# An adaLN block with a mixture of experts on one Trainium2 core: the hand-written orders around block 7's routing, and where the load of expert 1's weights stands

## The reference

```python
h = _layernorm(x, axis=-1) * (1 + cb) + sb
scores = jax.nn.softmax(xt @ router_w, axis=-1)              # 8 experts
expert_weights, expert_idx = jax.lax.top_k(scores, TOP_K)     # 2 of them
h = gelu(einsum('td,edf->tef', xt, w1)) * einsum('td,edf->tef', xt, v1)   # f = 704
y = einsum('tef,efd->ted', h, w2)
out = sum(expert_weights * y[chosen], axis=1) + bias
x = x + gb * out
```

## Time and profile before

| | us |
|---|---|
| median of 3 runs | 848.93 |
| lowest, highest | 848.23, 850.63 |
| profiled execution, its time | 848.34 |
| its span, first to last instruction | 846.2 |
| TensorE busy in the span | 818.6 (97%) |
| VectorE, GpSimd, ScalarE busy | 557.7, 485.8, 367.9 |
| mean granted TensorE clock | 0.996 of full |

### The profile page before, as it was taken

The page is one execution under the profiler, slowest core; times in us unless marked ns, Lnnn a source line. Parts: engine busy times, 40 slices in busy tenths (PEclk is TensorE's granted clock), DMA queues, the critical chain, the costliest instruction groups (busy, mean ns, idle before and its releaser), DMA issues.

```text
span 846.2 us, 18804 instructions
## 1 busy us (share of the span) xinstructions
PE 818.6 (97%) x5006; PEld 724.6 (86%) x5007; DVE 557.7 (66%) x1534; ACT 367.9 (43%) x681; POOL 485.8 (57%) x454
## 2 busy tenths in 40 slices
PE   8899999999999999978999999999999999999995
PEld 4679898988889879757999999999999999999994
DVE  6788777878876848775555655555655565565553
ACT  5884657565564525534224234224233242342221
POOL 2353645868685877569645646537537465383332
PEclk9999999999999999999999999999999999999998
DMA  8141050303021172327532432523324322222221
GB/s 281 34 113 50 2 181 9 119 26 102 14 90 45 58 233 62 142 78 199 153 47 40 137 45 37 150 44 113 68 38 137 51 37 44 38 38 38 38 45 25
DMA packets 49983, 67.64 MB, mean 80 GB/s; under 512 B 4944, under 2 KB 44240, under 8 KB 49936
## 3 DMA queue, kind: packets, MB, share of 16 engines
q1 hardware_dynamic: 36272, 47.71, 18.4%
q0 software_dynamic: 13664, 19.35, 12.2%
HBM read 43.51 MB, written 23.54 MB: 79 GB/s over the span
## 4 chain that ended last, share of the span: by engine, by line
PE 87%; POOL 3%; DVE 3%; issue 1%; ACT 1%; DMA 1%; another core or an unknown queue 0%; ACTq 0%; DVEq 0%; POOLq 0%
PE ps L614 24%; PE ps L616 24%; PE ps L615 24%; PE ps L776 5%; PE ps L742 2%; PE ps L715 1%; POOL routed L2009 1%; DMA out_rows<-y_moe,tok_moe 1%; PE ps L819 1%; PE ps L818 1%; PE ps L660 1%; PE ps L702 1%; PE ps L632 1%; PE ps L667 1%; POOL out_rows L2031 1%
## 5 line engine op out<-in xcount | busy, mean ns | idle before, releaser
L614 PE MATMUL ps<-split,xT_moe_hi 128*128 (+2 forms) x426 | 165.5, 388 | 0.1
L616 PE MATMUL ps<-split,xT_moe_hi 128*128 (+2 forms) x426 | 160.1, 376 | 0.0
L615 PE MATMUL ps<-split,xT_moe_lo 128*128 (+2 forms) x426 | 159.8, 375 | 0.0
L2021 POOL TENSOR_TENSOR y_moe<-y_moe 128x256 f32<-128x256 f32 x69 | 65.9, 956 | 122.8 <-DVE y_moe L1653 122.6
L1174 ACT ACTIVATE hidT_hi<-ps 128x768 fp32r<-128x768 f32 x70 | 56.9, 813 | 177.7 <-PE ps L776 168.6
L2031 POOL DMA_INDIRECT out_rows<-y_moe,tok_moe x71 | 111.1, 1564 | 28.9 <-issue 22.5
L1168 ACT ACTIVATE gelu_moe<-ps 128x704 f32<-128x704 f32 x71 | 53.8, 758 | 133.6 <-PE ps L616 126.9
L614 PE MATMUL ps<-split,hidT_hi 128*128 (+1 forms) x355 | 99.9, 281 | 1.3 <-DVE y_moe L1653 0.7
L615 PE MATMUL ps<-split,hidT_lo 128*128 (+1 forms) x355 | 100.1, 282 | 0.0
L616 PE MATMUL ps<-split,hidT_hi 128*128 (+1 forms) x355 | 99.9, 281 | 0.0
L1970 POOL TENSOR_TENSOR hid_lo<-hf_sb,hid_hi 128x512 fp32r<-128x512 f32 x48 | 67.1, 1399 | 50.8 <-ACT hid_hi L1146 50.7
(11 more groups left out here) (232 smaller groups left out, 1993.9 us busy)
## 6 DMA issues: line engine op xcount, KB each, us to landing
raw<-in_w SPq DMA_DIRECT2D x9, 1408.0 KB
x_moe<-routed SPq DMA_DIRECT2D x74, 132.5 KB
raw<-in_w SPq DMA_DIRECT2D x9, 640.0 KB
x_again<-in_x SPq DMA_DIRECT2D x8, 512.0 KB
out_rows<-x_again SPq DMA_DIRECT2D x8, 512.0 KB
x_sb<-in_x SPq DMA_DIRECT2D x7, 512.0 KB, 3.9
gu_raw<-in_gu_t SPq DMA_DIRECT2D x1, 1536.0 KB, 8.9
raw<-in_w SPq DMA_DIRECT2D x18, 64.0 KB
```

What stands on the lines that cost most here:

```text
L614: pe.matmul(dst, a_hi, b_hi, start=first, stop=False)
L615: pe.matmul(dst, a_lo, b_hi, start=False, stop=False)
L616: return pe.matmul(dst, a_hi, b_lo, start=False, stop=last)
L2021: g.tensor_tensor(y_moe[:, t.slot, 0, :], y_moe[:, t.slot, 0, :], y_moe[:, t.slot, 1, :], ALU.add)\
```

## The change

Six lists are edited; no computation is added or taken away but fills. SyncE: the load of expert 1 goes from ahead of the table's wait to behind the rows of tiles 5 to 8. TensorE: the fills in this part become fewer and stand elsewhere (27 before, 13 after); ranks 6 and 7 move ahead; hidden transposes and second product of tile 4 go ahead of tile 5's row transposes, out of `tile_step`. ScalarE: `router_exp(6)` goes ahead of gelu 1, the splits of expert 0 and the copies of block 7 change places with gelus. VectorE: `slots(6)` and `weigh(6)` follow block 7's statistics, `count(7)` moves behind `slots(7)` and `weigh(7)`, and the low splits of expert 0 move to the end.

```diff
@@ SyncE
             store_base(NBLK - 2)
-            load_weights(sp, 1, RAW_SLOT)
             sp.wait_ge(tab_ready, 1)
...
             for n in range(EARLY, EARLY + SLOTS):
                 load_by_table(Tile(n))
+            load_weights(sp, 1, RAW_SLOT)
             store_base(NBLK - 1)
             load_weights(sp, 2, 0)
@@ TensorE, tile_step
-                hid_transposes(t.near(-1))
-                if t.n > EARLY and not final(t):
-                    x_transposes(t.near(1))
+                if t.n > EARLY:
+                    hid_transposes(t.near(-1))
+                    if not final(t):
+                        x_transposes(t.near(1))
                 first_products(t, e)
                 if t.n == EARLY:
                     x_transposes(t.near(1))
-                second_product(t.near(-1), PICKED if t.n == EARLY else pe.snap(kept, min_val=0, max_val=E - 1))
+                else:
+                    second_product(t.near(-1), pe.snap(kept, min_val=0, max_val=E - 1))
@@ TensorE, list
             first_products(Tile(1), PICKED, AB[2:])
-            pe.wait_ge(gelu_r, 2)
-            fill(0, 3)
+            rank_tokens(6)
             x_transposes(Tile(2))
             second_product(Tile(0), PICKED)
-            rank_tokens(6)
+            pe.wait_ge(gelu_r, 2)
+            fill(0, 8)
             hid_transposes(Tile(1))
             first_products(Tile(2), PICKED, AB[:2])
-            pe.wait_ge(hid_r, 2)
-            fill(2, 4)
             h2_transposes(7, 0)
             first_products(Tile(2), PICKED, AB[2:])
             h2_transposes(7, 1)
+            x_transposes(Tile(3))
             router_logits(7)
-            x_transposes(Tile(3))
             second_product(Tile(1), PICKED)
-            fill(RING, 5)
+            rank_tokens(7)
             hid_transposes(Tile(2))
-            rank_tokens(7)
             first_products(Tile(3), PICKED, AB[:2])
+            first_products(Tile(3), PICKED, AB[2:])
             count_all()
-            first_products(Tile(3), PICKED, AB[2:])
-            fill(RING, 4)
+            x_transposes(Tile(4))
             second_product(Tile(2), PICKED)
-            x_transposes(Tile(4))
-            fill(RING, 4)
-            table_transposes()
-            pe.wait_ge(gelu_r, 4)
-            fill(0, 7)
             hid_transposes(Tile(3))
             first_products(Tile(4), PICKED, AB[:2])
+            table_transposes()
             first_products(Tile(4), PICKED, AB[2:])
             second_product(Tile(3), PICKED)
+            hid_transposes(Tile(4))
+            second_product(Tile(4), PICKED)
+            pe.wait_ge(gelu_r, 5)
+            fill(0, 5)
             x_transposes(Tile(5))
@@ ScalarE, list
             hidT_split(Tile(0))
+            router_exp(6)
             gelu(Tile(1))
             xT_split(Tile(2))
-            router_exp(6)
-            hidT_split(Tile(1))
             split_hi(act, 0, 0)
             split_hi(act, 0, 1)
+            hidT_split(Tile(1))
             h2_copy(7, 0)
+            gelu(Tile(2))
             h2_copy(7, 1)
-            gelu(Tile(2))
             xT_split(Tile(3))
+            split_hi(act, 0, 2)
             router_exp(7)
-            split_hi(act, 0, 2)
...
             gelu(Tile(4))
+            hidT_split(Tile(4))
             xT_split(Tile(5))
-            hidT_split(Tile(4))
@@ VectorE, list
             norm2_stats(7)
+            slots(6)
+            weigh(6)
             multiply(Tile(1))
             xT_rest(Tile(2))
             norm2_centre(7)
             norm2_scale(7)
-            slots(6)
-            weigh(6)
+            hidT_rest(Tile(1))
             gate_y(Tile(0))
             count(6)
-            hidT_rest(Tile(1))
             multiply(Tile(2))
             choose(7)
-            count(7)
             xT_rest(Tile(3))
-            take_gates(Tile(2), expert)
             slots(7)
             weigh(7)
             hidT_rest(Tile(2))
+            count(7)
             gate_y(Tile(1))
+            take_gates(Tile(2), expert)
+            multiply(Tile(3))
+            xT_rest(Tile(4))
             table()
-            split_lo(v, 0, 2)
-            xT_rest(Tile(4))
-            multiply(Tile(3))
-            split_lo(v, 0, 0)
-            table_out()
             hidT_rest(Tile(3))
             gate_y(Tile(2))
-            split_lo(v, 0, 1)
+            table_out()
             multiply(Tile(4))
-            xT_rest(Tile(5))
+            split_lo(v, 0, 0)
             take_gates(Tile(3), expert)
             gate_y(Tile(3))
+            hidT_rest(Tile(4))
+            split_lo(v, 0, 1)
+            xT_rest(Tile(5))
             take_gates(Tile(4), expert)
-            hidT_rest(Tile(4))
+            split_lo(v, 0, 2)
             take_gates(Tile(5))
```

## The result

The changed kernel takes 859.99 us (median of 4, 857.44 to 860.83) against 849.78 (848.23 to 850.8) of the kernel before on the same chip: ratio 1.0120, 95% interval 1.0094 to 1.0145, so 10 us slower, outside the forecast's range. The profiled execution took 860.83 us (span 858.7), the slowest of its four, and that of the kernel before 848.34, so the two traces lie 12.5 us apart and the medians 10.2.

The account below looks back on a forecast made before the run. Bound: the chain to tile 6's hidden transposes, then TensorE alone. Load issued 384.85 + 1.7 = 386.5, + 10.3 = 396.8, + 4.5 = 401.3 against 402.09, 0.8 us sooner: 848.1 against 848.93; 8-in-10 range 845.4 to 851.8.

Parts of the forecast that it names:

- late signals: TensorE's h2, logit and rank signals beside scatter 6: delay between 0 and 3.4 us, taken as 1.7.
- 0.3 planned: Second product 3 on TensorE was to wait 0.3 us for `gate_y(2)`.
- The load: Expert 1's load: issued at 386.5, landing 10.3 us later, then 4.5 us to tile 6's hidden transposes.
- Clock: Rival, chance 0.20: TensorE's clock falls in new gaps before second product 4 or hidden 6; total 850 to 852 us.
- mark of error: Sign of being wrong: a TensorE clock below 1.00 between 377 and 405 us.
- price of 2 to 4 us: Cost the clock rival, chance 0.20, put on top of the sum for half clock after a gap.
- the 5 or more: Sign of being right: ScalarE idle 5 us or more before L395, released by a DMA.
- The load is hidden: Rival, chance 0.10: load lands by 393, ScalarE doesn't wait, 4.3 to 6 us faster, 843 to 844.6.
- The gain of the order: Scatter 7 and tile 5's rows come sooner; some 3.5 us of the gain is lost waiting for the load.
- 396.1 without the load's wait: When TensorE would reach tile 6's hidden transposes if the load held nothing; 397.8 with late signals.
- planned 2.5: TensorE's wait ahead of second product 4, planned at 2.5 us.
- Choice 7: Block 7's choice on VectorE: takes 1.9 us, ends about 361.7 against 361.81; over 1 us off means wrong.

Follow-up runs that it names:

- e14: Changed kernel with at most two scatters in flight in blocks 6 and 7: 853.10 us, ratio 1.0036 to the kernel before.
- e3: Changed kernel with matmuls on ones added in TensorE's gaps: 855.53 us, ratio 1.0109 to the kernel before.
- e2: Kernel before with only the load of expert 1 moved behind the rows of tile 8: 852.26 us, ratio 1.0051.
- e12: Changed kernel with early load, early low split piece, two scatters in flight at most in blocks 6 and 7, no added matmuls: 848.77 us, ratio 0.9984.
- e8: Changed kernel with only one scatter of block 7 in flight at a time: 858.23 us, ratio 1.0111 to the kernel before.
- e11: Kernel before with only a limit of two scatters in flight in blocks 6 and 7: 852.29 us, ratio 1.0021.
- e1: Changed kernel with the load of expert 1 issued early again: 853.44 us, ratio 1.0079 to the kernel before.
- e13: Kernel before without its 27 fills between tiles 1 and 4: 848.98 us, ratio 1.0000.

## Why the prediction was wrong

- **The failed step: late signals, sized at 1.7 us.** The prediction took half of 3.4, between one row that showed 3.4 and the dense steps that showed 0.3. The changed kernel has 2.3 at the logits, 3.9 at second product 3 (6.2 in ScalarE's row), and 1.3 at the table, where VectorE waits 1.07 us on its own instruction before: 7.2 us on the path beyond the 0.3 planned, more than its upper bound of 3.4, since that was a bound for one signal, and the order has several behind each other. Limiting the scatters, and nothing else, gave back 7 of 10 us (e14). The load went out at 399.35 instead of 386.5, 12.8 us late, landed in 1.0 us less than forecast, and tile 6 came 11.8 us late.
- **The order was the multiplier.** The prediction saw scatter 6 come to lie over the logits. It did not ask the same of scatter 7, moved to 368 to 378, over tile 3's hidden transposes and the table. In the kernel before the same transposes lay beside scatter 7 with the signal on time, and second product 3, at 382.48, had slack; in the changed order `gate_y(2)`, second product 3, the transposes and second product 4 hang on each other with no slack.
- **Clock.** The rival was right in its mechanism and in sign, and its own mark of error, a clock below 1.00 between 377 and 405, came. By counting durations at half clock in the profiled execution (products of tile 3 1.6 us more, second products 3 and 4 1.7 each, transposes and `fill`s 1.5) it holds 6.6 us (6.5 by these rounded terms). With 7.2 of late signals and logits 1.1 us later that makes 14.9, against the 14.5 us by which x of tile 5 (397.13, forecast 382.65) is late. But the gaps that it follows are mostly made by the late signals. Filling them gave 0.9 us by the ratios, 4 at most (e3), and with most signals on time less was at half clock (0.92 and 0.98 in e14, 0.88 and 0.54 in the changed kernel). The prediction's price of 2 to 4 us was fair for the gap at tile 6 (2.1 in e2, 1.5 here); the larger part came ahead of it, behind gaps that weren't planned. The Trainium skill (TensorE: Matmul & The Clock Gate, What's actually happening) has the throttled state as the default; by that rule the rival was likelier than 0.20, and the trace agrees.
- **The load.** Mechanism and terms held: 9.3 us for the load (10.9 in e2, 10.2 in e14), 4.4 to 4.5 us behind it, and a TensorE wait of 2.0, 4.3 and 2.9 us. It costs 3.5 to 4.5 us in all. ScalarE idled 2.88 us ahead of L395, not the 5 or more that the prediction had as a sign of being right (5.17 in e2). The step from `take_gates` to the load, 384.2 to 384.85, has no row in the prediction; here it is 0.66 us (398.69 to 399.35). The prediction balanced the load against a gain of the order of which the larger part never came. "The load is hidden" is refuted by each of these rows.
- **The gain of the order.** Rows of tile 5 in time, yes; scatter 7 from 368.01 instead of 369.89, 1.9 us sooner. The prediction's 396.1 without the load's wait has two parts: x of tile 5 at 382.65 instead of 386.15, and 13.45 us from there to tile 6 instead of 15.94. The second came (13.69 in e12). The first didn't, even with most signals on time: x of tile 5 starts at 386.10 in e14 and 388.96 in e12. In e14 TensorE waits 1.5 us for `seen_b`, behind the late ranks, and 3.2 us ahead of second product 4 (planned 2.5), which then takes 3.5 us at half clock instead of 2.0. So with the load early the new order is worth 0.0016 (e12), 1.4 us and not clear of nothing, where the prediction had 4.3 to 6.
- **Choice 7** was to end at 361.7 and ended at 365.0, which the prediction had as a sign of being wrong: logits 1.1 us later than worked out, and 2.3 us of late signal. The 1.1 us aren't the change's: this execution reached tile 0's hidden transposes 0.4 us later, and tile 1's products ran partly at half clock (0.72 in 342 to 348), 0.6 us longer up to the logits than in e8 and e12, which have the same order there at 1.00.
- **Left open:** why TensorE's signals wait for scatters, why the dense steps with the same scatters show at most 0.3 us, whether the low split beside scatter 7 kept tile 3's signal in time in the kernel before, and why two in flight give 0.1 us at one hand-over and 1.6 to 2.7 at others. Split kernels of V (GpSimd's sums moved away) weren't tried.

## What to carry to other kernels

When the trace has one unexplained wait, find what runs beside it and multiply: a change that strings several hand-overs beside that same thing pays it at each. Ask for each moved DMA not only who waits for it but whose signals it will run beside. Keep slack, another piece of work, between an engine's signal and the instruction that needs its result; matmuls on ones kept the clock up here, but bought no time where TensorE would have waited anyway. And set the marks of two traces from a common point ahead of the change before comparing them.

## What the hardware showed that was not expected

- With several indirect scatters of 128 rows in flight, signals from TensorE reached ScalarE and VectorE up to 6.2 us late; up to 2.7 us with two in flight (e11), 0.04 with one, 0.03 with none. With the same scatters but one of them issued over 2.51 us it was 0.04 (kernel before).
- A subtraction of VectorE of 128x1408 took 4.81 us instead of 1.63 beside GpSimd's elementwise work (e1), and GpSimd's sum 2.76 instead of 0.74; a scatter's issue took 2.51 instead of 0.96 beside such a subtraction (kernel before).
- In a gap of 4.3 us the clock fell to half, and it stayed there for another 4.5 us, though TensorE was busy from the gap's end (e2); 27 matmuls on ones that keep the clock at 1.00 instead of 0.81 were worth nothing in time (e13).
